# Residual tokens turned on VectorE and by DMA, added in the next image's second stage

## What is computed

```python
x = h_in + proj(softmax(q.T @ k / 16) @ v)      # q, k, v from group_norm(x); N = 1024 tokens, C = 256
t = _to_tokens(x)                               # 1024 x 256
t = t + _L1_attn_ref(_ln_t(t))                  # softmax of squared cosines, times the normalised tokens
t = t + _L1_ffn_ref(_ln_t(t), weight, bias)     # sign weights, clip to [-1, 1], rounded to sevenths
x = _from_tokens(t, x)                          # back to 256 x 1024
```

## Time and profile before

| | us |
|---|---|
| Three runs | 1740.52, 1741.99, 1742.3; median 1741.99 |
| The profiled execution | 1741.46 |
| its span in the profile | 1739.7 |
| mean granted TensorE clock in it, as a share of full speed | 0.994 |
| TensorE, VectorE, ScalarE, GpSimd busy | 1665.7, 1385.1, 992.2, 767.2 |
| DMA | 259.86 MB, its queue 49.1% of 16 engines' span |

### The profile page before, as it was taken

One profiled execution on the slowest core, in us unless ns is written; L12 is line 12 of the kernel. 1 busy time (PEld: TensorE's weight loads), 2 busy tenths in 40 slices (PEclk: granted clock), 3 DMA queues, 4 the chain that ended last, 5 costly groups with the idle time before them and its releaser, 6 DMA issues.

```text
span 1739.7 us, 33604 instructions
## 1 busy us (share of the span) xinstructions
PE 1665.7 (96%) x10994; PEld 1509.5 (87%) x10994; DVE 1385.1 (80%) x2687; ACT 992.2 (57%) x1586; POOL 767.2 (44%) x1206
## 2 busy tenths in 40 slices
PE   6999999999999999999999999999999999999996
PEld 5898889989899898898988898898998989989896
DVE  6778688787878878788787887878788787887875
ACT  3555655656565564655657456565655656556572
POOL 1262634625345253543626346253552635336161
PEclk9999999999999999999999999999999999999998
DMA  4544546355464554546445463554545545463441
GB/s 119 166 126 157 148 133 201 123 168 150 137 173 133 181 150 142 153 135 203 133 156 156 132 195 121 169 155 136 172 128 182 159 141 152 135 195 109 158 136 58
DMA packets 218750, 259.86 MB, mean 149 GB/s; under 512 B 30176, under 2 KB 188256, under 8 KB 218720
## 3 DMA queue, kind: packets, MB, share of 16 engines
q1 hardware_dynamic: 218720, 259.48, 49.1%
HBM read 138.81 MB, written 120.59 MB: 149 GB/s over the span
## 4 chain that ended last, share of the span: by engine, by line
PE 62%; DVE 12%; issue 8%; DMA 8%; ACT 5%; SPq 3%; POOL 2%; DVEq 0%; ACTq 0%; POOLq 0%
PE wide L465 21%; DMA e_scratch<-x_norm 6%; PE turn L628 3%; PE turn L679 3%; PE wide L558 3%; PE wide L560 3%; PE wide L559 3%; PE turn L630 3%; PE narrow L628 3%; PE narrow L630 3%; PE turn L629 3%; PE narrow L629 3%; PE narrow L560 3%; PE narrow L558 3%; PE narrow L559 3%
## 5 line engine op out<-in xcount | busy, mean ns | idle before, releaser
L465 PE MATMUL wide<-xn_hi,prob 128*128 128x512 f32 x1024 | 300.4, 398 | 2.7 <-DVE prob L1121 2.7
L822 ACT ACTIVATE expo<-wide,neg_max 128x1024 f32<-128x1024 f32 x128 | 142.7, 1115 | 183.0 <-DVE neg_max L1131 182.0
L465 PEld LDWEIGHTS wide<-xn_hi,prob 128*128 128x128 f32 x1024 | 187.4, 189 | 42.9 <-DVE prob L1121 3.1
L829 ACT ACTIVATE prob<-e_back 128x1024 fp32r<-128x1024 f32 x112 | 118.5, 1058 | 132.4 <-DMA e_back<-e_scratch 132.4
L1503 POOL TENSOR_TENSOR carrier_p<-ones 128x1 f32<-128x1 f32 x60 | 11.7, 195 | 405.4 <-DVE y_sb L1247 402.9
L1140 DVE STREAM_TRANSPOSE x_norm<-expo 128x1024 f32<-128x1024 f32 x112 | 139.3, 1244 | 46.8 <-ACT expo L822 45.0
L1487 POOL TENSOR_TENSOR prob<-expo,prob 128x128 fp32r<-128x128 f32 (+6 forms) x112 | 146.5, 1320 | 53.0 <-DVE prob L1180 53.0
L1145 DVE TENSOR_TENSOR prob<-e_back,prob 128x1024 fp32r<-128x1024 f32 x112 | 136.0, 1214 | 38.4 <-ACT prob L829 38.3
L1131 DVE TENSOR_REDUCE neg_max<-wide 128x1 f32<-128x1024 f32 x128 | 156.0, 1219 | 11.7 <-PE wide L465 10.8
L465 PE MATMUL wide<-xn_lo,prob 128*128 128x512 f32 x512 | 161.2, 395 | 0.0
L558 PE MATMUL wide<-prob 128*128 128x256 f32 x512 | 149.9, 293 | 4.7 <-DVE prob L1145 4.7
(11 more groups left out here) (181 smaller groups left out, 5197.1 us busy)
## 6 DMA issues: line engine op xcount, KB each, us to landing
e_scratch<-x_norm SPq DMA_DIRECT2D x112, 512.0 KB, 3.6
e_back<-e_scratch SPq DMA_DIRECT2D x448, 128.0 KB, 2.9
x_raw<-in_x SPq DMA_DIRECT2D x32, 512.0 KB, 3.7
e_back<-in_x SPq DMA_DIRECT2D x64, 256.0 KB, 5.0
out<-y_sb SPq DMA_DIRECT2D x64, 256.0 KB, 3.1
ln_scratch<-x_norm SPq DMA_DIRECT2D x30, 512.0 KB, 2.6
expo<-ln_scratch SPq DMA_DIRECT2D x120, 128.0 KB, 2.8
e_scratch<-x_norm SPq DMA_DIRECT2D x32, 448.0 KB, 2.6
```

The source lines that it names most:

```text
L465: mm = pe.matmul(o, lhsT, r, start=first and i == 0, stop=last and i == len(parts) - 1)
L822: act.activation(expo[:, n % DEEP], wide[n % 2][:, :], ACT.Exp, bias=neg_max[:, n:n + 1], accum_out=row_sum1[:, n:n + 1]).then_inc(e1_made, 1)
```

## The change

The residual tokens no longer go over TensorE. VectorE turns them as 32x32 squares (`tok_turn`) into `ln2`, which is free by then; it stands where `output` stood. SP sends both halves to a scratch tensor in HBM and fetches them back in turned order, behind `fetch(b, 6)`. `output(f, hf)` now adds them from SBUF, as one operation of 128x1024 a half, in the second stage: the first half before `residual1(b, 7)`, the second behind it. The stores move behind `send2(b, 0)` and `fetch2(b, 0)`. The last image keeps the old way (`output_last`).

Beside it the lists are reordered. ScalarE: `layer_norm2` of rows 4 to 7 ahead of the two `query_hi`; both `ln2T_hi` earlier. VectorE: `ln2_turn(f, 1)` between the two `query_lo`, `value_lo(b, 1)` ahead of `x_tokens`, `row_max(b, 0)` ahead of `x_tokens(b, 1)`, both `ln2T_lo` ahead, `gn_sums(b+1, 1)` and `clip(f, 0)` later. GpSimd: `layer_norm1` and `lengths` of rows 4 and 5 ahead of `e2_lo(b, 0)` and `e2_lo(b, 1)`; all second-norm coefficients ahead of `bias_quads(b+1, 1)`.

```diff
+        tok_scratch = nc.dram_tensor("tok_scratch", (2, P, N), F32).ap()
+        tok_in = tok_scratch.rearrange("h (q c) (b f) -> h b c q f", q=SQ, b=SQ)
+        tok_squares = [ln2[:, HT * hf:HT * (hf + 1), :].rearrange("p n c -> p (n c)") for hf in range(2)]
@@ SP
+            def send_tok(f, hf):
+                sp.wait_ge(tok_turned, 2 * f + hf + 1)
+                sp.dma_start(tok_scratch[hf], tok_squares[hf]).then_inc(tok_written[hf], 16)
+            def fetch_tok(f, hf):
+                sp.wait_ge(tok_written[hf], 16 * (f + 1))
+                back = tok_squares[hf].rearrange("p (q f) -> p q f", q=SQ)
+                for c in range(SQ):
+                    sp.dma_start(back[c * Q:(c + 1) * Q], tok_in[hf, c]).then_inc(tok_landed[hf], 16)
...
                 send2(b, 0)
+                if f is not None:
+                    store(f, 0)
                 fetch2(b, 0)
+                if f is not None:
+                    store(f, 1)
...
                 if f is not None:
-                    store(f, 0)
-                    store(f, 1)
+                    for hf in range(2):
+                        send_tok(f, hf)
+                    for hf in range(2):
+                        fetch_tok(f, hf)
@@ TensorE front
-                if f is not None:
-                    pe.wait_ge(y_made, 4 * f + 4)
-                    turn_t(f, 0)
                 product1(b, 0)
                 scores1(b, 5)
-                if f is not None:
-                    pe.wait_ge(out_made, 2 * f + 1)
-                    turn_t(f, 1)
...
                 if f is not None:
-                    pe.wait_ge(out_made, 2 * f + 2)
+                    pe.wait_ge(y_made, 4 * f + 4)
                 turn_last_e1(b)
@@ ScalarE front
-                query_hi(b, 0)
                 if f is not None:
                     layer_norm2(f, 4)
                     layer_norm2(f, 5)
-                query_hi(b, 1)
+                query_hi(b, 0)
                 if f is not None:
                     layer_norm2(f, 6)
                     layer_norm2(f, 7)
+                query_hi(b, 1)
                 value_hi(b, 0)
                 value_hi(b, 1)
+                if f is not None:
+                    ln2T_hi(f, 0)
                 exp1(b, 0)
-                if f is not None:
-                    ln2T_hi(f, 0)
                 exp1(b, 1)
+                if f is not None:
+                    ln2T_hi(f, 1)
...
                     ffn_out(f, 0, reuse)
-                if f is not None:
-                    ln2T_hi(f, 1)
@@ VectorE
+            def tok_turn(f, hf):
+                dve.wait_ge(t2_made, NT * f + HT * (hf + 1))
+                for k in range(KC):
+                    last = dve.transpose(
+                        tok_squares[hf].rearrange("p (c k n t) -> p k n c t", c=SQ, k=KC, t=Q)[:, k],
+                        tok[:, HT * hf:HT * (hf + 1), tile(k)].rearrange("p n (c t) -> p n c t", t=Q))
+                last.then_inc(tok_turned, 1)
...
+            def output(f, hf):
+                dve.wait_ge(tok_landed[hf], 16 * SQ * (f + 1))
+                dve.wait_ge(q_made, 2 * f + hf + 1)
+                y = y_sb[:, hf].rearrange("p k (q f) -> p k q f", q=SQ)
+                dve.tensor_tensor(y, tok_squares[hf].rearrange("p (q k f) -> p k q f", q=SQ, k=KC), y, ALU.add
+                                  ).then_inc(out_made, 1)
@@ VectorE front
                 query_lo(b, 0)
-                if more:
-                    gn_sums(b + 1, 1)
+                if f is not None:
+                    ln2_turn(f, 1)
                 query_lo(b, 1)
                 value_lo(b, 0)
+                value_lo(b, 1)
...
                 x_tokens(b, 0)
+                row_max(b, 0)
+                if f is not None:
+                    ln2T_lo(f, 0)
+                e1_turn(b, 0, f)
+                row_max(b, 1)
                 x_tokens(b, 1)
-                row_max(b, 0)
-                if f is not None:
-                    ln2_turn(f, 1)
-                e1_turn(b, 0, f)
-                value_lo(b, 1)
-                row_max(b, 1)
-                if f is not None:
-                    ln2T_lo(f, 0)
                 e1_turn(b, 1, f)
                 value_lo(b, 2)
                 value_lo(b, 3)
+                if more:
+                    gn_sums(b + 1, 1)
+                if f is not None:
+                    ln2T_lo(f, 1)
+                row_max(b, 2)
                 if f is not None:
                     clip(f, 0)
-                row_max(b, 2)
-                if f is not None:
-                    ln2T_lo(f, 1)
                 e1_turn(b, 2)
...
-                    output(f, 0)
+                    tok_turn(f, 0)
                 e1_turn(b, 4)
...
-                    output(f, 1)
+                    tok_turn(f, 1)
                 row_max(b, 6)
...
                 cosT_lo(b, 1)
+                if f is not None:
+                    output(f, 0)
                 residual1(b, 7)
+                if f is not None:
+                    output(f, 1)
                 cosT_lo(b, 2)
@@ GpSimd front
                 layer_norm1(b, 1)
                 lengths(b, 1)
+                layer_norm1(b, 2)
+                lengths(b, 2)
                 e2_lo(b, 0)
                 e2_lo(b, 1)
-                layer_norm1(b, 2)
-                lengths(b, 2)
                 value_lo(b, 1)
@@ GpSimd back
-                layer_norm2(b, 0)
+                for g in range(N2):
+                    layer_norm2(b, g)
                 if more:
                     bias_quads(b + 1, 1)
-                for g in range(1, N2):
-                    layer_norm2(b, g)
```

More of the change, by code:

```diff
@@ L288, in build @@
         out_made = sem("out_made")
+        tok_turned = sem("tok_turned")
+        tok_written = [sem("tok_written0"), sem("tok_written1")]
+        tok_landed = [sem("tok_landed0"), sem("tok_landed1")]
         stored = [sem("stored0"), sem("stored1")]
@@ L416, in fetch2, with second @@
                     sp.dma_start(back[q * Q:(q + 1) * Q], source[q]).then_inc(e2_landed[e2_slot(g)], 16)
-            def second(b):
+            def second(b, f):
                 send2(b, 0)
+                if f is not None:
+                    store(f, 0)
                 fetch2(b, 0)
+                if f is not None:
+                    store(f, 1)
                 send2(b, 1)
@@ L444, in _ @@
             reload_quads(1)
-            second(0)
+            second(0, None)
             with sp.Fori(1, B - 1) as b:
@@ L449, in _ @@
                 reload_quads(b + 1)
-                second(b)
+                second(b, b - 1)
             front(B - 1, B - 2)
-            second(B - 1)
+            second(B - 1, B - 2)
             store(B - 1, 0)
@@ L682, in ffn, with turn_t @@
                 mm.then_inc(y_up, 1)
-            def turn_t(f, hf, places=PLACES):
+            def turn_t(f, hf, places):
                 for k in range(KC):
@@ L930, in front @@
                     layer_norm2(f, 7)
+                query_hi(b, 1)
                 value_hi(b, 0)
                 value_hi(b, 1)
-                exp1(b, 0)
                 if f is not None:
                     ln2T_hi(f, 0)
+                exp1(b, 0)
                 exp1(b, 1)
+                if f is not None:
+                    ln2T_hi(f, 1)
                 value_hi(b, 2)
@@ L1256, in quantise, with output_last @@
                                   ).then_inc(q_made, 1)
-            def output(f, hf, places=PLACES):
-                dve.wait_ge(tT_up, 2 * f + hf + 1)
+            def output(f, hf):
[4 more added lines that the diff above has]
+                                  ).then_inc(out_made, 1)
+            def output_last(f, hf, places):
+                dve.wait_ge(tT_up, hf + 1)
                 dve.wait_ge(q_made, 2 * f + hf + 1)
@@ L1281, in front @@
                 x_tokens(b, 0)
-                x_tokens(b, 1)
                 row_max(b, 0)
                 if f is not None:
-                    ln2_turn(f, 1)
+                    ln2T_lo(f, 0)
                 e1_turn(b, 0, f)
-                value_lo(b, 1)
                 row_max(b, 1)
-                if f is not None:
-                    ln2T_lo(f, 0)
+                x_tokens(b, 1)
                 e1_turn(b, 1, f)
@@ L1397, in _ @@
             quantise(f, 0)
-            output(f, 0, LAST)
+            output_last(f, 0, LAST)
             clip(f, 1)
             quantise(f, 1)
-            output(f, 1, LAST)
+            output_last(f, 1, LAST)
         @block.gpsimd
```

## The result

Six runs of the changed kernel gave a median of 1748.63 us (1747.17 to 1749.58), six of the kernel before 1741.47 (1734.4 to 1743.81). The ratio is 1.0045, with an interval of 1.0027 to 1.0063: **slower by 0.45%**, where 1738 and a gain of 0.2% had been forecast. The profiled execution took 1749.58 us; its span is 1747.9 and its mean granted TensorE clock 0.989 (0.994 before).

The account below looks back on a forecast made before the run. TensorE was taken as the bound, with five short waits and engines that must follow. A turn: 1.7 + 0.2 + 0.1 - 2.1, then 0.3 behind, net 0.2 us; with 0.6 for the first front 1741.5 - 3.6 = 1738, range 1700 to 1756.

Parts of the forecast that it names:

- What bounds the kernel: Steady loop: TensorE busy 102.82 of 105.5 us, five short waits of 2.7; other engines must come earlier too.
- Part 1: Front: two blocks of 8 token transposes leave TensorE, 1.75 us a turn; VectorE's squares replace its additions evenly.
- Part 2: Front: reordering removes waits of 0.31, 0.65 and 0.43 us; everything down to row 5's statistics comes 1.7 us early.
- waits for exponentials: VectorE's list from `row_max(b, 2)` to `e1T_lo(b, 1)`: these grow by about 0.3 us, within 12.6 us altogether.
- Part 3: Second stage: the two additions with two SBUF operands hold GpSimd's gapless coefficient chain 1.05 us each, 2.1 a turn.
- the 0.2 and 0.1 of the forecast: Chain up to `turn_cos(b, 3)`: 0.2 us gained from GpSimd's new order and 0.1 us that was to spare.
- Part 4: DMAs behind `fetch(b, 6)`: tokens land before the additions want them, stores get in nobody's way; priced at nothing.
- The sum: Per turn: -0.1 us at `turn_cos(b, 3)`, some 0.3 gained behind it, net 0.2 faster; 1738 us altogether.
- the 0.6 given to it: First front: 0.6 us gained, as it has the better order and no additions.
- the third: Front: quantiser passes and `e1T_lo(b, 0)` exclude each other, VectorE held up to 1.1 us; 1755 us, chance 0.14.
- The first rival: Second stage: the additions don't hold GpSimd, 2.3 us a turn gained; 1706 us, chance 0.18 (held once: 1722, 0.12).

Follow-up runs that it names:

- experiment 8: The changed kernel with `gn_deviation` ahead of `clip(f, 0)`, both token additions behind `e2T_lo(b, 5)` and both stores at the end of SP's second stage: 1718.81 us.
- experiment 7: The kernel before with all reordered lists, residual tokens still turned on TensorE and added from PSUM, and `gn_deviation` ahead of `clip(f, 0)`: 1707.76 us.
- experiment 1: The changed kernel with each token addition replaced by a VectorE transpose of the same size and place, reading one SBUF operand: 1714.04 us.
- experiment 4: The kernel before with all reordered lists of the change, residual tokens still turned on TensorE and added from PSUM in the front: 1718.13 us.
- experiment 3: The changed kernel with `gn_deviation` moved ahead of `clip(f, 0)` and `e1_turn(b, 2)`: 1738.8 us.
- experiment 2: The changed kernel with the additions moved behind `e2_turn(b, 5)` and `e2T_lo(b, 5)`, and the stores to the end of SP's second stage: 1731.19 us.
- experiment 5: The kernel before with two unneeded 128x1024 VectorE operations, each with two SBUF operands, added in the second stage: 1769.92 us.

## Why the prediction was wrong, point by point

**What bounds the kernel**: right. TensorE's waits were the place to look, and what decides is whether the others follow: in experiment 8 they don't, and in experiment 7 the turn is nearly all TensorE.

**Part 1**: right by its size. TensorE is 1.5 to 2 us a turn less busy. Experiments 7 and 8, and 1 and 4, add that in this order these 1.75 us turn into waits. The wait for the group means came out at 0.31, where 0.2 at most was given.

**Part 2, "all that follows it comes 1.7 us early"**: this is the step that failed. Its beginning was right to the tenth: `row_max(b, 2)` was put at 893.3 and started at 896.08 less 2.84, 893.24. The walk from there was too short: it gave 12.6 us to `e1T_lo(b, 1)`, and it took 13.13 (896.08 to 909.21). It charged "waits for exponentials" with 0.3 more and asked of the quantiser only whether its passes would end ahead of `e1T_lo(b, 0)`. The nearer meeting was overlooked: `gn_deviation` stands between, its subtraction reads two SBUF operands, and it was held for 0.55 us (0.71 instead of 0.16). `e1T_lo(b, 1)` came at 906.37 instead of 905.9, `fetch(b, 6)` at 923.91 instead of 923.4, and the statistics of row 5 at 933.02 by the mark of before: **a gain of 1.2 us, not 1.7**, and this turn is a good one: in the median of 14 turns those statistics start 58.75 us behind `query_lo(b, 0)`, before 59.64, a gain of 0.9. Since the chain behind it has no slack, all of it reaches TensorE. In experiment 3 the median is 58.07, a gain of 1.6; it is faster by 9.8 us, and experiment 7 against experiment 4 by 10.4: the bulk of the 10.6 us between forecast and result. These differences hold the meeting and the better place of the four operations together.

**Part 3**: right. The additions were priced at 1.05 each, 2.1 a turn; they hold GpSimd by 0.88 and 0.98, and a cast of VectorE that the delay brings beside `ln_v` (943.83) holds it for 0.17 more, together the 2.03 of experiment 1, 15 times 30 us. From row 5's statistics to `turn_cos(b, 3)` it took 12.75 us (935.86 to 948.61), before 10.95 (934.21 to 945.16): 1.8 longer, which is 2.1 less the 0.2 and 0.1 of the forecast. Right for the places of the change only: experiment 2 shows that the same addition elsewhere costs VectorE 1.1 us instead. The new wait of over 2 us at `turn_cos(b, 3)` came too (2.06).

**Part 4**: right. No addition waited for a landing, and no row shows `fetch2` or the stores in the way.

**The sum**: a forecast of minus 0.2 us a turn stands against plus 0.94 measured over 14 turns, 16 us in all. In medians of these turns, from `query_lo(b, 0)` to row 5's statistics 0.9 was gained instead of 1.7, and 0.7 of what is missing comes back in experiment 3 (its turns take 105.5 us, not 106.2). From there to `turn_cos(b, 3)` 1.85 was lost instead of 1.8, and behind it 0.18 gained (34.63 us, before 34.81) instead of 0.3. That makes a turn 0.8 longer. The fall of the clock, which no step had, adds 0.3 (4 us over these turns), and one long turn of the kernel before (107.53 from its `query_lo(1, 0)`) takes 0.15 off. Against it stand 2.7 us that the opening gained beyond the 0.6 given to it, and 1.5 at the end, beyond the 0.2 of the last turn. 16.0 - 2.7 - 1.5 is 11.8 by spans, which is the 1749.58 of the profiled execution less 1738, within 0.2. That experiment 3 gives just the forecast 1738 is in part luck: its opening is better than forecast and its clock still falls four times.

**The rivals**: the third had the right kind of mechanism, a meeting with the quantiser after a later `clip(f, 0)`, with 0.14 and 1755 us; it put it at the subtraction `e1T_lo(b, 0)`, which in the changed kernel runs at 902.17, 1.5 us after the last pass, and is not held. In experiments 3 and 7, where the clip comes later and this subtraction earlier, it is: 1.51 to 1.53 us in all 14 turns. The first rival's 1706 (GpSimd not held) is what experiment 1 would come to if the 8 to 10 us of the meeting were taken off its 1714, an estimate that no run tests.

**What stays open**: what the meeting at `gn_deviation` costs without the better place; and why the clock falls after six of 15 equal waits and not after the others; in experiment 5 it fell after five of eleven waits of 1.98 us and after none of four of 1.71. No kernel was run to tell that apart. Also open is what exactly made the opening 3.3 us shorter; experiments 4 and 7 have it too (their `query_lo(1, 0)` stands at 130.04 and 130.6), so it comes with the order.

## What to carry to other kernels

Walk every instruction of VectorE that reads two SBUF operands, the two-column ones too, and its casts against what GpSimd runs at that time: either side can be the one held, for up to the whole of the other's length. Moving an addition's operand from PSUM to SBUF changes what it collides with, though its own time stays nearly the same (two of 677 ns before, one of 1.22 us now), so its new place belongs beside a stretch where GpSimd is idle or waiting. Work taken off the busiest engine was worth nothing here, because the engines that feed it came no earlier: the reordering with the work left on TensorE gave 1.3%, and with `gn_deviation` first 2.1%.

## What the runs showed of the hardware

How long an operation was held didn't depend on its own size. One on 128x2 was stretched from 0.69 to 1.57 us (GpSimd, beside a 1.22 us addition) and from 0.16 to 0.71 (VectorE, beside a 1.05 us rounding pass), in each case to about the end of the other. A cast of 128x512 with one SBUF input was stretched from 0.42 to 1.37.

The granted TensorE clock fell from 1.00 to 0.50 for 3.3 us after a wait of 2.06 us, in six of 15 turns with the same wait and the same work around it; in the kernel before, whose longest wait in the earlier trace rows is 0.97, the turn read is at 1.00, and no stretch of 3 us between 130 and 1690 us is under 0.95. Waits of 1.38 to 1.46 us in twelve turns of experiment 2 were never followed by a fall. A wait of two us can so cost nearly one more, which no sum over the waits has in it.
